# Attention and feed-forward on one core: softmax sums joined through DRAM in place of a TensorE product

## What is computed

```python
cq = rms_norm(x @ w_qa.T, q_a_ln_w)                 # 2048 x 384
q_nope, q_pe = split(cq @ w_qb.T)                   # per head 128 and 64 wide, q_pe turned by rope
ckv_l, k_pe = rms_norm(ckv[..., :128]), rope(ckv[..., 128:])
scores = (q_nope . k_nope + q_pe . k_pe) * scale    # causal
attn = softmax(scores)
x = _layernorm(x + (attn @ v) @ w_o.T)
x = _layernorm(x + (x @ (weight * scale_weight[:, None]).T + bias))
```

## Time and profile before

| | us |
|---|---|
| median of 2 runs | 1629.78 (1628.8 to 1630.75) |
| profiled execution | 1629.23 |
| its span, first to last instruction | 1627.5 |
| PE busy in the span | 1589.4 |
| DVE busy | 1455.7 |
| ACT busy | 1112.6 |
| POOL busy | 995.5 |
| mean granted TensorE clock | 0.994 |

### The profile page before, as it was taken

One profiled execution on the slowest core, in us unless ns is written; L12 is line 12 of the kernel. 1 busy time (PEld: TensorE's weight loads), 2 busy tenths in 40 slices (PEclk: granted clock), 3 DMA queues, 4 the chain that ended last, 5 costly groups with the idle time before them and its releaser, 6 DMA issues.

```text
span 1627.5 us, 27022 instructions
## 1 busy us (share of the span) xinstructions
PE 1589.4 (98%) x8149; PEld 1347.9 (83%) x8149; DVE 1455.7 (89%) x2706; ACT 1112.6 (68%) x2067; POOL 995.5 (61%) x1001
## 2 busy tenths in 40 slices
PE   7999999999999999999999999999999999999887
PEld 6788888888888888888888888888888888888766
DVE  4666899899999999989999999999999999999996
ACT  4555776676667676766677666766677777776774
POOL 4333666565666666656666566666656666666796
PEclk9999999999999999999999999999999999999999
DMA  7994422222321322223221412123223112111322
GB/s 214 352 344 140 133 91 66 77 73 71 131 90 39 123 66 85 72 85 130 80 64 46 149 53 92 51 79 124 67 83 104 59 53 72 53 46 59 123 98 91
DMA packets 112169, 163.94 MB, mean 101 GB/s; under 512 B 13600, under 2 KB 83488, under 8 KB 109984
## 3 DMA queue, kind: packets, MB, share of 16 engines
q1 hardware_dynamic: 105296, 125.86, 23.8%
q0 software_dynamic: 4864, 16.26, 3.2%
q10 hardware_dynamic: 1872, 20.19, 3.0%
HBM read 101.19 MB, written 61.08 MB: 100 GB/s over the span
## 4 chain that ended last, share of the span: by engine, by line
PE 89%; POOL 3%; DVE 3%; DMA 2%; issue 2%; ACT 1%; DVEq 0%; ACTq 0%; SPq 0%; POOLq 0%
PE rows L1495 25%; PE bank L1495 12%; PE rows L1537 8%; PE bank L1513 7%; PE bank L1514 7%; PE bank L1516 7%; PE rows L1458 5%; PE bank L1458 4%; PE bank L1537 3%; PE bank L1471 2%; PE rows L401 2%; PE rows L1471 2%; DMA wq<-wq_dram 1%; PE rows L1557 1%; POOL split_p L1728 1%
## 5 line engine op out<-in xcount | busy, mean ns | idle before, releaser
L1728 POOL TENSOR_TENSOR split_p<-pool,split_p 128x512 fp32r<-128x512 f32 x544 | 704.7, 1297 | 434.6 <-ACT split_p L1624 433.0
L1624 ACT CAST split_p<-pool 128x512 fp32r<-128x512 f32 x544 | 338.4, 622 | 109.8 <-PE bank L1516 79.8
L1907 DVE TRANSPOSE_TENSOR_REDUCE parts<-pool 128x16 f32<-128x512 f32 x544 | 377.2, 693 | 0.0
L1900 DVE TENSOR_TENSOR pool<-bank,pool 128x512 f32<-128x512 f32 x544 | 368.2, 677 | 2.2
L1617 ACT ACTIVATE pool<-pool 128x512 f32<-128x512 f32 x544 | 342.5, 630 | 19.9 <-DVE pool L1900 18.3
L1495 PE MATMUL rows<-q_c,key_c 128*128 128x512 f32 x1089 | 310.7, 393 | 0.0
L1612 ACT COPY pool<-rows 128x512 f32<-128x512 f32 x320 | 186.3, 582 | 89.8 <-PE rows L1495 89.8
L1495 PEld LDWEIGHTS rows<-q_c,key_c 128*128 128x128 f32 x1089 | 198.3, 188 | 36.3
L1495 PE MATMUL rows<-q_pe,key_pe 128*128 128x512 f32 x726 | 224.6, 390 | 0.0
L1513 PE MATMUL bank<-split_p,val 128*128 128x512 f32 x544 | 218.6, 402 | 1.3 <-ACT o_sum L1630 1.3
L1516 PE MATMUL bank<-split_p,val 128*128 128x512 f32 x544 | 213.1, 392 | 3.7 <-POOL split_p L1728 3.7
(11 more groups left out here) (201 smaller groups left out, 2427.7 us busy)
## 6 DMA issues: line engine op xcount, KB each, us to landing
q_pe<-pe_dram SPq DMA_DIRECT2D x128, 128.0 KB, 2.6
y_dram<-y SPq DMA_DIRECT2D x62, 256.0 KB, 2.1
cq<-cq_dram SPq DMA_DIRECT2D x19, 768.0 KB, 4.8
y<-y_dram SPq DMA_DIRECT2D x48, 256.0 KB, 3.2
pe_dram<-by_sin SPq DMA_DIRECT2D x32, 256.0 KB, 2.1
pe_dram<-by_cos SPq DMA_DIRECT2D x32, 256.0 KB, 2.2
cq_more<-cq_dram SPq DMA_DIRECT2D x10, 768.0 KB, 4.9
table<-table_dram SPq DMA_DIRECT2D x56, 128.0 KB, 2.7
```

The source lines that it names most:

```text
L1624: nc.scalar.copy(split_p[:, n % 2, 0, :], slot(n)).then_inc(p_hi, 1)
L1728: nc.gpsimd.tensor_tensor(split_p[:, n % 2, 1, :], slot(n), stored(split_p[:, n % 2, 0, :]), ALU.subtract).then_inc(p_lo, 1)
L1900: nc.vector.tensor_tensor(slot(n), MAXES, slot(n), ALU.add).then_inc(shifted, 1)
L1907: nc.vector.tensor_reduce(parts[:, t, :], in_blocks(slot(n)), AX.X, ALU.add, apply_transpose=True).then_inc(summed, 1)
```

## The change

`fold_sum` is gone. In its place SP stores `row_sum` (128 x 16, 8 KB) in DRAM and loads it four times, each time into 32 partitions of `all_sums` (128 x 4 x 16), so that every partition has all four parts. `spread_sum` waits for the 4 loads and adds the parts on DVE with one reduce (128x64 to 128x16), then takes the reciprocal as before. The bank that `fold_sum` had is now `spread_sum`'s, whose waits DVE makes. The two steps, `store_sum` and `load_sum`, have places of their own, and some thirty numbers of `AT` are others. The ones that this text speaks of stand in the diff.

```diff
+        self.sum_dram = nc.dram_tensor("sum_dram", (2, P, 4 * HG), F32, kind="Internal").ap()
...
-    'sum': -5.6, 'rotate': 11.9, 'fold_max': 38, 'reduce_sum': -5, 'fold_sum': 46, 'spread_sum': 38, 'normalise': 33.1,
+    'sum': -8.6, 'rotate': 10.9, 'fold_max': 51, 'reduce_sum': -7.15, 'spread_sum': 38, 'normalise': 33.1,
+    'store_sum': -7, 'load_sum': 19,
-    'f_in': -27, 'f_z_statistics': 72.85, 'w_slot': 5,
+    'f_in': -48, 'f_z_statistics': 81.85, 'w_slot': 7.15,
...
-            yield ("fold_sum", it - 2)
-    elif what == "fold_sum":
+            yield ("store_sum", it - 2)
+    elif what == "store_sum":
         yield ("reduce_sum", it)
+        if it >= 2:
+            yield ("load_sum", it - 2)
+    elif what == "load_sum":
+        yield ("store_sum", it)
+        if it:
+            yield ("spread_sum", it - 1)
     elif what == "spread_sum":
-        yield ("fold_sum", it)
+        yield ("load_sum", it)
...
-AUX_USES = ("q", "pe", "y", "fold_max", "fold_sum", "turn", "linear")
+AUX_USES = ("q", "pe", "y", "fold_max", "spread_sum", "turn", "linear")
...
+            def store_sum(it):
+                sp.wait_ge(sum_reduced, it + 1)
+                if it >= 2:
+                    sp.wait_ge(sum_loaded, 64 * (it - 1))
+                sp.dma_start(m.sum_dram[it % 2], row_sum[it % 2]).then_inc(sum_stored[it % 2], 16)
+
+            def load_sum(it):
+                sp.wait_ge(sum_stored[it % 2], 16 * (it // 2 + 1))
+                if it:
+                    sp.wait_ge(totalled, it)
+                for b in range(4):
+                    sp.dma_start(all_sums[32 * b:32 * b + 32, :, :], m.sum_dram[it % 2].rearrange("(a i) n -> i a n", a=4)
+                                 ).then_inc(sum_loaded, 16)
...
-            def fold_sum(it):
-                u = ("fold_sum", it)
-                shared(u)
-                if it == 0:
-                    pe.wait_ge(fold_made, 2)
-                pe.wait_ge(sum_reduced, it + 1)
-                pe.matmul(aux(u)[:, 0:4 * HG], fold[:, :], row_sum[it % 2], start=True, stop=True).then_inc(sum_folded, 1)
...
-                    dve.wait_ge(sum_folded, it - 1)
+                    dve.wait_ge(sum_stored[it % 2], 16 * (it // 2))
...
             def spread_sum(it):
-                u = ("fold_sum", it)
-                dve.wait_ge(sum_folded, it + 1)
-                nc.vector.reciprocal(inv_sum[it % 2], aux(u)[:, 0:4 * HG]).then_inc(inv_done, 1)
+                u = ("spread_sum", it)
+                dve.wait_ge(sum_loaded, 64 * (it + 1))
+                nc.vector.tensor_reduce(total[:, :], all_sums[:, :, :].rearrange("p a b -> p b a"), AX.X, ALU.add
+                                        ).then_inc(totalled, 1)
+                dve.wait_ge(totalled, it + 1)
+                nc.vector.reciprocal(inv_sum[it % 2], total[:, :]).then_inc(inv_done, 1)
                 dve.wait_ge(inv_done, it + 1)
+                shared(u)
```

More of the change, by code:

```diff
@@ L768, in window_slot @@
     return FIRST[2 * s] + j * (keys(2 * s) + keys(2 * s + 1)) // 3
-AT = {'scores': -2, 'max': 7.85, 'shift': -35, 'exp': -20, 'hi': -14, 'sum': -5.6, 'lo': -15.65, 'values': 1, 'reduce_max': 19, 'widen_max': 24, 'fold_max': 38, 'join_max': 46, 'spread_max': -26, 'reduce_sum': -5, 'copy_out': 10.15, 'fold_sum': 46, 'spread_sum': 38, 'normalise': 33.1, 'o_hi': 44, 'o_lo': 49.25, 'y': 76, 'add_y': 60.15, 'q': 9, 'q_hi': 45.85, 'q_lo': 19.8, 'pe': 6, 'rope': 16.85, 'round_pe': 63, 'store_pe': 55, 'load_pe': 66, 'f_in': -27, 'f_statistics': 0, 'f_centre': 6, 'f_invert': 17, 'f_turn': 25, 'f_copy_x': 30, 'f_rest_x': 30.05, 'f_scale': 46, 'f_add_bias': 51, 'f_linear': 63, 'f_z': 70, 'f_z_statistics': 72.85, 'f_z_invert': 85, 'f_apply': 101, 'f_out': 106.05, 'f_ready': -4, 'f_ready_last': 7, 'f_pace': 2, 'f_first': 3, 'w_slot': 5, 'rotate': 11.9, 'values_first': 10.0}
+AT = {'scores': -1.85, 'max': 7.85, 'shift': -34, 'exp': -20, 'hi': -14.15, 'sum': -8.6, 'lo': -14.8, 'values': 1, 'reduce_max': 18, 'widen_max': 25, 'fold_max': 51, 'join_max': 50, 'spread_max': -39, 'reduce_sum': -7.15, 'copy_out': 9.15, 'spread_sum': 38, 'normalise': 33.1, 'o_hi': 46.85, 'o_lo': 49.25, 'y': 74, 'add_y': 60.15, 'q': 11, 'q_hi': 57.85, 'q_lo': 19.8, 'pe': 6, 'rope': 18.85, 'round_pe': 81, 'store_pe': 55, 'load_pe': 6, 'f_in': -48, 'f_statistics': 0, 'f_centre': 8, 'f_invert': 17, 'f_turn': 25, 'f_copy_x': 30, 'f_rest_x': 30.05, 'f_scale': 46, 'f_add_bias': 51, 'f_linear': 63, 'f_z': 69, 'f_z_statistics': 81.85, 'f_z_invert': 88, 'f_apply': 102, 'f_out': 106.05, 'f_ready': -17, 'f_ready_last': 7, 'f_pace': 2, 'f_first': 3, 'w_slot': 7.15, 'rotate': 10.9, 'values_first': 9.0, 'store_sum': -7, 'load_sum': 19}
 SPREAD, SCORES_AT, COPIES, SHIFT, EXP, ROUND, VALUES, READ, MAX, USE_AT, FFN_TURN, FFN_LINEAR, FFN = range(13)
@@ L813, in timetable @@
         yield 13 * value_slot(it, 0) + AT["spread_max"], 0, ("spread_max", it)
-        for what in ("reduce_sum", "copy_out", "fold_sum", "spread_sum", "normalise", "o_hi", "o_lo", "y", "add_y"):
+        for what in ("reduce_sum", "store_sum", "load_sum", "copy_out", "spread_sum", "normalise", "o_hi", "o_lo", "y", "add_y"):
             yield 13 * last_value(it) + AT[what], 0, (what, it)
@@ L859, in readers @@
         return [("join_max", use[1])]
-    if use[0] == "fold_sum":
-        return [("spread_sum", use[1]), ("normalise", use[1])]
+    if use[0] == "spread_sum":
+        return [("normalise", use[1])]
     if use[0] == "y":
@@ L1137, in attention_phase @@
         wide_max = sb("wide_max", [P, 2, 4 * 4 * HG])
+        all_sums = sb("all_sums", [P, 4, 4 * HG])
+        total = sb("total", [P, 4 * HG])
         stats = sb("stats", [P, 8, 4 * HG])
@@ L1184, in attention_phase @@
         sum_reduced = sem("sum_reduced")
-        sum_folded = sem("sum_folded")
+        sum_stored = [sem(f"sum_stored{n}") for n in range(2)]
+        sum_loaded = sem("sum_loaded")
+        totalled = sem("totalled")
         fold_made = sem("fold_made")
@@ L1389, in _ @@
                     given["stores"] += at[0] < output_of(DIRECT)
+                elif what == "store_sum":
+                    store_sum(*at)
+                elif what == "load_sum":
+                    load_sum(*at)
                 elif what == "store_pe":
@@ L1573, in _ @@
                     values(*at)
-                elif what == "fold_sum":
-                    fold_sum(*at)
                 elif what == "q":
```

20 lines of the change are left out of this document (19 added, 1 removed).

## The result

The changed kernel takes 1665.29 us (median of 2 runs, 1664.77 to 1665.81) against 1629.78 before: 1.0218 times as long, 95% interval 1.0199 to 1.0237. So it is slower; whether by 2% or more the interval leaves open. The prediction was 1621, with 1613 to 1633 as its range. The profiled execution took 1664.77 us, its span 1663.1.

A forecast was written before the change was run, and what follows sets the result against it. PE was taken to bound the kernel up to 1500 us, DVE after it. From 1629.2, less 14.2 for folds, plus 4.0 behind large loads and 2.0 at the end: 1621 us, range 1613 to 1633.

The forecast's parts named there:

- Places moved elsewhere: Moved `fold_max`, `sum` and `rotate`: taken as 0, bounds -4 and +4, from PE's own gaps of 4.9 us.
- signs of being wrong: DVE waiting over 1 us in most passes, PE gaps of 20 us or more, or over 5 us longer after the last score.
- What goes: Folds on PE: 59 of 64 at 0.24 us each, 14.2 us off, or 7.7 by the lower bound of 0.13.
- fourth rival: A fold on PE costs only 0.13 us, less than the starts say: 1627.5 us in all; chance 0.05.
- What comes on DVE: Added reduce in `spread_sum`: 0.24 us a pass, 15 us in all, fitting DVE's idle time; spare falls to 1.07 us a pass.
- The end: After 1500 us: 1.2 us on DVE for five passes, 0.8 for DMAs on SyncE; 2.0 together, bounds -3 and +10.
- The round trip: Store 2.1 plus loads 3.9, 6.0 us from `reduce_sum`; six passes wait 0.7 us, nearly covered by slack.
- Behind large loads: Sums queued on SyncE behind `wq` or tokens: five places 2 us late, PE losing 0.8 each, 4.0 us; bounds 0 and 10.
- The queue: SyncE issuing the sums' store and four loads: no separate cost for issues or traffic in the sum.
- second rival: DVE becomes the bound, waiting on loaded sums at `spread_sum` in every pass: 1639 us; chance 0.12, of it 0.04 over 1662.

The follow-up runs named there:

- e3_new_places: The kernel before, sums still joined by TensorE's product, with all the changed kernel's numbers in `AT`: 1658.42 us, 1.0176.
- e7_lo: The changed kernel with only `lo` put back to -15.65, so GpSimd does it ahead of `rotate` again: 1631.68 us, 1.0017 to before.
- e1_rotate: The changed kernel with only `rotate` put back from 10.9 to 11.9: 1635.82 us, 1.0041 to before.
- e4_no_join: The kernel before without `fold_sum` and nothing joining the sums, an addition of the same size standing for the reciprocal: 1619.89 us, 0.9936.
- e15_extra_reduce: The kernel before with an unused reduce of 128x64 to 128x16 on DVE ahead of each reciprocal: 1631.17 us, 1.0012.
- e10_unused_dma: The kernel before with the sums' store and four loads issued on SyncE and nobody using the data: 1629.39 us, 1.0004.

## Why the prediction was wrong

**The step that failed** is "Places moved elsewhere": "`rotate` earlier ... Taken as 0, bounds -4 and +4". It measured +29 us (`e3_new_places` over before), and undoing it at one number gives back 33.6 (`e7_lo`) or 29.5 (`e1_rotate`). The bounds were read from PE's present gaps, 4.9 us. Gaps that PE has now bound what a move can win; they say nothing of what it can lose. The row that would have told was in the same list of waits: GpSimd stood 50.6 us before `by_cos` for DVE's `by_sin`, 25 times and up to 7.4 us, and the list has only 4.3 us of PE for GpSimd, at `o_lo`. To move an instruction with such a wait past another is to put that wait in front of it. An estimate was to be had from two numbers: the mean wait, 50.6 / 25 = 2.0 us, less the slack of 0.57 us that I had read for just such a `lo`, times 25, makes 36 us. That it comes so near the 33.6 is in part luck: the wait that it estimates was 22.9 us, and GpSimd's own wait didn't stay at 50.6 but grew to 111.8. It would have told of a loss of tens of us, far outside the bounds of 4. The prediction goes through the orders of DVE, SyncE and PE, and never GpSimd's. One of its own signs of being wrong did come: gaps of PE of 20 us or more (36.6).

**What goes**: 14.2 us was counted, 9.6 measured (`e4_no_join`, which also takes away the waits for the folds; 7.7 to 13.2 by its interval). The distance of starts, 0.24 us a fold, is too much; the lower bound of 0.13 us, 7.7 us in all, lies at the interval's edge. In PE's busy time a fold was worth 0.20 us, and a part of that went in new waits. So the fourth rival was partly right. The Trainium skill's 25 ns for a short matmul ("TensorE: Matmul & The Clock Gate", "Back-to-back issue gap") makes an estimated 3.2 us of the 128; the run shows 75 ns for each. The two aren't the same thing: by the same section the figure is for a matmul by itself, and in a stream of weight loads and matmuls both set the distance. The prediction held the bare figure against matmuls with weight loads, so its "the trace does not agree" says too much.

**What comes on DVE**: taken as hidden; it cost 2 us (`e15_extra_reduce`). About 1.2 us of that was in the prediction, as part of "The end". DVE's spare of 1.07 us a pass is a mean: PE's idle time between the first score and the last is 6.4 us in that run, 4.9 before.

**The round trip**: 6.0 us was forecast from the end of `reduce_sum` to full data. In 19 of the 64 passes of the changed kernel it is 4.3 to 4.7. The DMA rows after (count, KB each, median us from issue to landing):

```profile
all_sums<-sum_dram SPq DMA_DIRECT2D x256, 8.0 KB, 1.8
...
sum_dram<-sums SPq DMA_DIRECT2D x64, 8.0 KB, 1.4
```

The store lands in 1.4 us and a load in 1.8, where larger transfers of before gave 2.1 and 2.6. So the parts were too large. Over all 64 passes the way takes 5.9 us in the median and up to 11.7, since other DMAs stand in between; the forecast total is right for the middle by luck. The six shortest passes, where 0.7 us of wait was forecast, have none from their own length: in every pass 5.3 us or more go by before DVE is at the reduce.

**Behind large loads**: right in its mechanism. DVE waits for the sums in 14 places (forecast: 10 to 15 passes), the longest where SyncE is busy with something else. The two places that the prediction worked out are among them: in the tenth pass the tokens land 10.3 us after their issue at 423.69, the sums' store, issued behind them, takes 3.8 us to land, and the loads go out at 434.19. But DVE waits only 0.39 us in it and 0.84 in the fifteenth, for a forecast 1.4 and 1.7. The three longest waits are elsewhere: 4.28 in the first pass, and 1.22 in the eleventh, where loads of `q_pe` and of tables are issued ahead of the sums' DMAs; and 2.01 in the fifty-first, where SyncE comes to the loads 2.1 us after the store has landed. The size was off. Without `rotate`'s effect, `e7_lo` stands 11.8 us over `e4_no_join`; less the 2 us of the added reduce, some 10 us are left for the round trip and the other moved places, where the sum had 4.0 and 2.0. The rooms of "0.6 to some 2 us, of which I take 1.2" were not there in the first pass, where 4.28 us on DVE became 3.96 us on PE. How much of the 10 us is the round trip is known from one side: 5.5 go with three issues fewer. The rest was not split.

**The queue**: taken as free, and it is, as far as can be measured (`e10_unused_dma`, 1.0004, 0.9994 to 1.0013).

**The end**: +2.0 forecast, +1.2 measured, within the bounds of -3 and +10. The feed-forward's moved numbers cost nothing that shows.

**The sum again**, with measured terms on 1629.4: -9.6 for the folds, +2 for the reduce, +10 for the round trip and smaller moves, 1632 in all, and +33.6 for the order on GpSimd: 1665. It closes by construction, since the 10 is a remainder and the 33.6 a difference to the changed kernel itself; the 9.6 and the 2 were measured in the kernel before. The second rival, the one on the slow side, had the wrong mechanism for the time it gave: the sums' wait on DVE is 12.4 us in attention, far from the 22 us and more on PE that it needed.

## What to carry to other kernels

An instruction that waits long on an in-order engine is harmless only for what stands behind it now. Before any step is moved, read the waits of every engine, the idle ones too, and ask for each large one whether the move puts something urgent behind it: here one crossing of two steps, made by one number of some fifty, cost 34 us in the changed kernel, and in the old one a move that crossed three kinds of steps cost 53. The gaps of the bounding engine bound what a move can win, not what it can lose.

A product that only joins a few numbers was worth 0.15 us here, less than its distance of starts said. A round trip through DRAM in its place pays only where its latency is covered: with one broadcast load in place of four, and `lo` ahead of `rotate`, it came out 3 us under the kernel before, with four loads never. Giving such a chain more time by moving all that hangs on it shifted the wait, here to the bank that `copy_out` frees and to the end of the program.

## What the runs showed of the hardware

- Small transfers on this path are quicker than the 128 x 512 ones: 1.4 us for an 8 KB store to DRAM, 1.8 us for each 8 KB load, and 4.3 to 4.7 us from the end of the reduce to full data, for a store and four loads with nothing ahead of them.
- 320 small DMAs more (64 stores, 256 loads) on a queue that also carries large loads made no measurable difference when nobody waited for them (1.0004, 0.9994 to 1.0013).
- After PE had stood for 3.96 us the granted clock was 0.50 for the next 4.6 us, and 12 matmuls took 5.3 us. So a wait of 4 us cost some 2.3 us again behind it. The same came behind a wait of 3.09 us (355.8 to 361.7 us, clock 0.50). This is a part of why PE's busy time rose although it had less to do. It isn't all: `e3_new_places`, with the same folds as before, has a busy time 9.0 us higher between the first score and the last, and only some 3.5 us at the half clock there. In the kernel before PE's longest listed wait in attention is 1.4 us, and its clock there was 1.00.
